# Two attention units and one layer product put into a written-out order at the end of a four-part residual kernel

## The chip, the cores and the metric

The kernel runs on one core of a Trainium2 chip. Its time is the device time of one execution in microseconds (us). The kernel before took 1401.56 us as the median of three runs (1401.19 to 1403.05). Engines are named as in the profile: PE (TensorE, matmuls), DVE (VectorE), ACT (ScalarE), POOL (GpSimd), SP (SyncE, which issues most DMAs; SPq is its queue).

## The reference

`x` is 8 sequences of 128 rows and 512 columns. Four residual layers follow each other:

```
x = x + L0(x)   gated MLP (512 -> 1376 -> 512) with low-rank adapters chosen per sequence
x = x + L1(x)   attention: 32 query heads, 8 key heads, D = 128, q/k RMS norm, rotary,
                512 cached keys from pages + 128 new keys, output projection Wo
x = x + L2(x)   x @ w_eff.T, w_eff = quantised weight (codebook, scales) + low-rank term, 512x512
x = x + L3(x)   x @ weight[adapter].T, one 512x512 matrix per sequence
```

## The kernel before

Every engine has its own queue, written by hand, and engines meet only by semaphores: a wait holds everything that stands behind it on that engine. All products are made in three parts: an operand is split into a high part (`*_h`, by an ACT copy to fp32r) and a low part (`*_l`, the rest, by a DVE or POOL subtraction), and PE multiplies h*h, h*l and l*h.

Layer L1 is cut into 64 units (8 key heads by 8 sequences, `Unit(k)`, k = 0 to 63). A unit goes through: projection of q, k, v; rotary (POOL); `scores(u, h)` for 4 query heads into the PSUM banks `sc0` and `sc1`; `mask_max(u, h)` on DVE, which adds the mask, writes `p_sb` and takes the row maximum (`top`); `shift(u, pair)` on DVE (`bias` from `top` and `rstd`); `exp(u, h)` on ACT; `transpose_p(u, c)` for 5 chunks of 128 keys into `ring0`/`ring1`; `high_pt` (ACT) and `low_pt` (DVE) that split each chunk; `attend(u, c)`, which sums the chunks in `o_ps`; `norm_o` (DVE, times `inv_wide`, which `lay_inv` on ACT writes from `inv_row`); `high_o` and `low_o`; `output(u)`, 12 matmuls into `proj_ps`; and `add_y(u)` (DVE), which adds to `x_sb`. `inv_row` comes by two DMAs of SP, one after the other: `put_inv` (2 KB to DRAM) and `spread_inv` (back to all partitions).

`step(u)` on each engine holds the work of up to four neighbouring units in a fixed order, and `run_steps` calls it for k = 2 up to 66, so that the last steps run with stages of units 62 and 63 alone. `before` is unit 62 and `last` is unit 63 in what follows.

Then come layers L2 and L3, sequence by sequence (b = 0 to 7): `turn_x` transposes `x_sb[b]`, `high_x2`/`low_x2` split it, `layer2(b)` is 12 matmuls, `add3(b)` adds, `turn_x(b, 1)` transposes again, `high_x3`/`low_x3` split, `layer3(b)` is 12 matmuls, `add4(b)` adds, and SP stores `out[b]`. The weights of L2 (1 MB, `w2_raw`) are loaded in one DMA behind the last `spread_inv` and split in one ACT and one DVE instruction; those of L3 are loaded for each sequence (1 MB, two buffers) and split by `high_w3` (ACT) and `low_w3` (DVE). PE waits for all of unit 63, its `add_y` too, ahead of `layer2(0)`.

In the trace the lines of these helpers are: scores L1490, transpose_p L1508, attend L1530, output L1546, L1549 and L1557, layer2 and layer3 L1235, turn_x L1657; mask_max L2021, shift L2037, low_pt L2054, norm_o L2062, low_o L2068, add_y L2074, add3 L2188, add4 L2193, low_w3 L2197, low_x2 L2202, low_x3 L2207, the split of w2 L1206 and L2212; exp L1003, high_pt L1014, high_v L1023, lay_inv L1032, high_o L1042, high_w3 L1190, high_x2 L1196, high_x3 L1202; on POOL rstd L726 and split_v (`vl`) L651; on SP put_inv L533, spread_inv L538, load_v L478 and the loads of w2, w3 and the stores L344. The trace leaves buffer numbers out (`sc`, `ring`), and calls w2 and w3 `w_raw`, `w_h`, `w_l`.

Of the kernel before, what the change touches and what calls it, by code (L numbers as in the profile page):

```python
# [106 lines left out]
def run_steps(step, first):  # L107


    for k in range(first, UNITS + DEPTH - 1):  # L110
        step(Unit(k))
# [17 lines left out]
def cond_resid_kernel(nc, ins, out):  # L129
    ctx = ExitStack()  # L130
    with ctx:
# [29 lines left out]
        down_ps = [o_ps[:, :], proj_ps[:, :]]  # L161
# [87 lines left out]
        p_sb = l1_sb("p_sb", [P, 6, KEYS])  # L249
# [92 lines left out]
        def _(sp):  # L342
# [230 lines left out]
        def _(pool):  # L573
# [164 lines left out]

            pool.wait_ge(S["iota_set"], 7)
            run_steps(step, 0)  # L740


        @block.scalar
        def _(act_e):
# [436 lines left out]
            run_steps(step, 2)  # L1181


            def high_w3(b):
                act_e.wait_ge(w3_load[b % 2], 16 * (b // 2 + 1))
                if b < 2:
                    act_e.wait_ge(S["y"], UNITS)
                else:
                    act_e.wait_ge(S["l3_done"], b - 1)
                act_e.activation(w3_h[:, b % 2, :, :], w3_raw[:, b % 2, :, :], ACT.Copy).then_inc(S["w3_hi"], 1)  # L1190

            def high_x2(b):
# [3 lines left out]
                act_e.activation(x2T_h[:, b % 2, :], ring[0][:, :], ACT.Copy).then_inc(S["xT_hi"], 1)  # L1196
# [7 lines left out]
            act_e.wait_ge(S["kv_done"], UNITS)  # L1204
            act_e.wait_ge(S["w2_in"], 48 * C + 16)
# [3 lines left out]
            for b in range(B):  # L1209
# [8 lines left out]
        def _(pe):  # L1218
# [414 lines left out]
            run_steps(step, 2)  # L1633


            def layer3(b):
# [17 lines left out]

            def turn_x(b, slot, name):
                for c in range(C):
                    i = nc.tensor.transpose(ring[slot][:, c * P:(c + 1) * P], x_sb[:, b, c * P:(c + 1) * P], ident[:, :])  # L1657
                i.then_inc(S[name], 1)

            pe.wait_ge(S["ptl"], UNITS * KC)  # L1660
            pe.wait_ge(S["y_added"], UNITS - B + 1)
            turn_x(0, 0, "xT_done")
            pe.wait_ge(S["y_added"], UNITS)
            for b in range(B):
                layer2(b)
                if b + 1 < B:
                    turn_x(b + 1, 0, "xT_done")
                if b:
                    layer3(b - 1)
                pe.wait_ge(S["x3_added"], b + 1)  # L1670
                turn_x(b, 1, "x3T_done")
# [4 lines left out]
        def _(dve):  # L1676
# [333 lines left out]
            def mask_max(u, h):  # L2010
# [7 lines left out]
                if u.back(ago):  # L2018
# [164 lines left out]
            run_steps(step, 2)  # L2183
# [103 lines left out]
```

## Time and profile before

| | before |
|---|---|
| median of 3 runs | 1401.56 us |
| the profiled execution | 1401.19 us, its span 1399.5 us, mean granted TensorE clock 0.996 |
| PE busy over the span | 1370.9 us (98%) |
| DVE / ACT / POOL busy | 1023.3 (73%) / 977.6 (70%) / 751.3 us (54%) |
| PE busy in 1310 to 1330 us | 15.81 of 20 us |
| PE busy in 1330 to 1340 us | 6.64 of 10 us |
| PE busy in 1340 to 1350 us | 6.99 of 10 us |
| PE busy in each 10 us from 1350 to 1390 us | 10.00 |

A time in the trace is counted from the start of the span; 1.69 us of the execution lie outside the span. The granted clock is given as a share of full speed; it is 1.00 in each of these stretches. An idle time in brackets stands at the instruction that ended it, with the releaser.

### The profile page before, as it was taken

Reading aid. Unit: us, or ns where it says so; the run is one execution under the profiler, and the core shown is the slowest. Engines: PE = TensorE matmul, PEld = TensorE weight load, DVE = VectorE, ACT = ScalarE, POOL = GpSimd, SP = SyncE. Lnnn points to the kernel's source line nnn. Section 1 sums busy time; section 2 is a strip of 40 time slices with the busy share of each in tenths; the row PEclk is TensorE's granted clock in tenths of the full one; section 3 lists DMA queues with packets and bytes.
Section 4 is the critical chain, followed back from the end, with each engine's and each line's share of the span. In section 5 each row is a group of like instructions: output and inputs, shape, how many; then the busy total and the mean of one; then the engine's idle time right before and its main releaser. Section 6 shows DMA issues by size and latency. Waiting matters only on the chain.

```text
span 1399.5 us, 26373 instructions
## 1 busy us (share of the span) xinstructions
PE 1370.9 (98%) x7830; PEld 1189.5 (85%) x7830; DVE 1023.3 (73%) x2112; ACT 977.6 (70%) x1986; POOL 751.3 (54%) x986
## 2 busy tenths in 40 slices
PE   9999999899999999999999999999999999999888
PEld 7878877788888888888888888888888888888766
DVE  4877776677777777777777777777777777777666
ACT  5757665577776677777777777777777777767643
POOL 5421323666765576557655665666566656655300
PEclk9999999999999999999999999999999999999999
DMA  7986889466334233524333334232424243332154
GB/s 194 269 282 178 273 269 286 110 140 170 92 64 106 61 91 65 118 68 96 64 106 62 91 61 106 61 92 63 115 59 108 62 110 71 82 61 61 32 187 151
DMA packets 256596, 165.80 MB, mean 118 GB/s; under 512 B 157398, under 2 KB 223575, under 8 KB 250951
## 3 DMA queue, kind: packets, MB, share of 16 engines
q1 hardware_dynamic: 249808, 142.48, 39.3%
q0 software_dynamic: 5376, 19.60, 5.1%
q10 hardware_dynamic: 1270, 2.04, 0.4%
q8 instruction: 64, 1.05, 0.3%
q14 instruction: 78, 0.63, 0.2%
HBM read 158.66 MB, written 38.94 MB: 141 GB/s over the span
## 4 chain that ended last, share of the span: by engine, by line
PE 77%; SPq 5%; POOL 4%; ACT 4%; DVE 4%; issue 3%; DMA 2%; POOLq 0%; ACTq 0%; DVEq 0%
PE proj_ps L1453 17%; PE sc L1490 15%; PE o_ps L1530 14%; PE ring L1508 9%; PE proj_ps L1546 4%; PE proj_ps L1549 4%; PE proj_ps L1557 4%; SPq L344 2%; PE o_ps L1235 2%; PE proj_ps L1235 2%; PE ring L1569 2%; SPq L381 2%; ACT wb L808 1%; POOL q_sin L680 1%; POOL q_cos L691 1%
## 5 line engine op out<-in xcount | busy, mean ns | idle before, releaser
L2054 DVE TENSOR_TENSOR pTl<-ring,pTh 128x512 fp32r<-128x512 f32 x320 | 215.2, 689 | 140.4 <-ACT pTh L1014 136.0
L1003 ACT ACTIVATE p_sb<-p_sb,bias,rstd 128x640 f32<-128x640 f32 x256 | 235.2, 919 | 57.5 <-DVE bias L2037 57.5
L726 POOL TENSOR_TENSOR rstd<-var,half_neg 128x4 f32<-128x4 f32 x64 | 68.8, 1076 | 304.9 <-DVE var L2086 304.9
L2021 DVE CUSTOM_DVE_ANT_0 p_sb<-sc,mask 128x640 f32<-128x640 f32 x256 | 206.0, 823 | 30.3 <-PE sc L1490 24.6
L1014 ACT ACTIVATE pTh<-ring 128x512 fp32r<-128x512 f32 x320 | 184.6, 600 | 29.5 <-PE ring L1508 27.9
L1508 PE MATMUL ring<-ident,p_sb 128*128 128x128 f32 x1280 | 181.5, 272 | 4.2 <-DVE pTl L2054 2.7
L1508 PEld LDWEIGHTS ring<-ident,p_sb 128*128 128x128 f32 x1280 | 152.8, 140 | 31.2 <-DVE pTl L2054 3.4
L1453 PE MATMUL proj_ps<-wh,xh 128*128 128x256 f32 (+1 forms) x484 | 168.6, 348 | 0.0
L1490 PE MATMUL sc<-kTh,qTh 128*128 128x320 f32 x512 | 163.0, 318 | 0.0
L1453 PE MATMUL proj_ps<-wl,xh 128*128 128x256 f32 (+1 forms) x484 | 161.9, 334 | 0.0
L1453 PE MATMUL proj_ps<-wh,xl 128*128 128x256 f32 (+1 forms) x484 | 161.7, 334 | 0.0
L1490 PE MATMUL sc<-kTh,qTl 128*128 128x320 f32 x512 | 158.4, 309 | 0.0
L1490 PE MATMUL sc<-kTl,qTh 128*128 128x320 f32 x512 | 158.1, 309 | 0.0
L1050 ACT ACTIVATE q_sb<-proj_ps 128x512 f32<-128x512 f32 x64 | 38.3, 598 | 170.9 <-PE proj_ps L1453 162.3
L634 POOL DMA_DIRECT2D v_pages<-in_v_cache x128 | 65.4, 511 | 142.6 <-issue 141.4
L680 POOL TENSOR_TENSOR q_sin<-q_sb,rope 128x256 f32<-128x256 f32 x128 | 92.6, 745 | 76.8 <-issue 72.5
L1530 PE MATMUL o_ps<-pTh,vh 128*128 128x512 f32 x256 | 116.9, 457 | 0.0
L1530 PE MATMUL o_ps<-pTl,vh 128*128 128x512 f32 x256 | 101.5, 397 | 0.0
L1490 PEld LDWEIGHTS sc<-kTh,qTh 128*128 128x128 f32 x512 | 96.6, 189 | 5.3
L1490 PEld LDWEIGHTS sc<-kTl,qTh 128*128 128x128 f32 x512 | 96.6, 189 | 5.2
L1530 PE MATMUL o_ps<-pTh,vl 128*128 128x512 f32 x256 | 101.0, 394 | 0.0
L1453 PEld LDWEIGHTS proj_ps<-wh,xh 128*128 128x128 f32 x484 | 91.4, 189 | 10.9
(264 smaller groups left out, 3633.8 us busy)
## 6 DMA issues: line engine op xcount, KB each, us to landing
v_pages<-in_v_cache POOLq DMA_DIRECT2D x128, 128.0 KB, 3.9
k_pages<-in_k_cache SPq DMA_DIRECT2D x128, 128.0 KB, 3.6
k_raw<-k_pages SPq DMA_DIRECT2D x256, 64.0 KB, 2.6
v_raw<-v_pages SPq DMA_DIRECT2D x64, 256.0 KB, 4.2
rope<-rope_dram SPq DMA_DIRECT2D x64, 256.0 KB, 3.8
inv_row<-inv_dram SPq DMA_DIRECT2D x64, 256.0 KB, 4.0
stage<-in_Wqkv SPq DMA_DIRECT2D x32, 384.0 KB, 4.9
w_raw<-in_WguT SPq DMA_DIRECT2D x19, 512.0 KB, 5.1
```

The costliest lines, as they stand in the source:

```text
L634: pool.dma_start(v_pages[b, j * PSIZE:(j + 1) * PSIZE, :, :].rearrange("s h d -> s (h d)"), ins["v_cache"][bass.ds(pg, 1), :, :, :].rearra ...
L680: pool.tensor_tensor(dst[:, :, s, :], src[:, :, 1 - s, :], tab[:, 1, s * 64:(s + 1) * 64].unsqueeze(1).to_broadcast([P, REP, 64]), ALU.mul ...
L726: pool.tensor_tensor(rstd[:, u.k % 2, 0:REP], var[:, u.k % 2, 0:REP], half_neg[:, 0:REP], ALU.pow).then_inc(S["q_pow"], 1)
L1003: act_e.activation(p_sb[:, p_slot(u, h), :], p_sb[:, p_slot(u, h), :], ACT.Exp, bias=bias[:, h:h + 1], scale=rstd[:, u.k % 2, h:h + 1], ac ...
L1014: act_e.activation(pTh[:, c, :], ring[c % 2][:, :], ACT.Copy).then_inc(S["pth"], 1)
L1235: i = mm(out, a, b, start=start and k == 0, stop=stop and k == last)
L1453: i = mm(proj_ps[:, 0:width], a[:, b, c, :], w[:, c, cols:cols + width], start=k == 0, stop=k == 3 * C - 1)
L1490: i = mm(score_ps[h % 2][:, s, 0:SPLIT], a[:, par, hs], w[:, par, ks], start=k == 0, stop=k == 2)
L1508: i = nc.tensor.transpose(ring[c % 2][:, h * P:(h + 1) * P], p_sb[:, p_slot(u, h), c * P:(c + 1) * P], ident[:, :])
L1530: i = mm(o_ps[:, :], a, w[:, c, :], start=c == 0 and k == 0, stop=c == KC - 1 and k == 2)
L2021: v.tensor_tensor_reduce(out=p_sb[:, p_slot(u, h), :].rearrange("p (s k) -> p s k", s=2), in0=score_ps[h % 2][:, :, 0:SPLIT], in1=mask[:, ...
L2054: v.tensor_tensor(pTl[:, c, :], ring[c % 2][:, :], pTh[:, c, :].bitcast(F32), ALU.subtract).then_inc(S["ptl"], 1)
```

## The change

The last steps (k = 64 to 66) are taken out of the loop on PE, DVE and ACT and written out by hand, mixed with the beginning of L2 and L3:

- PE: `scores(last, 2)` and `scores(last, 3)` come ahead of the third transposed chunk of unit 62; the transposes of `x_sb[0]` and `x_sb[1]` come ahead of unit 63's first chunk; `output(before)` comes behind the first two chunks of unit 63; `layer2(0)` comes ahead of `output(last)`.
- L2 writes to other PSUM banks: its transposes to the halves of `sc0` (two, in turn), its product to the first half of `sc1`. L3 keeps `proj_ps` and `ring1`.
- `p_sb` has 8 slots in place of 6, and unit 63 puts its heads 2 and 3 in the new ones, so that they need not wait until unit 62 is transposed.
- w2 is loaded by SP as soon as unit 63's k and v are projected, ahead of the steps 64 to 66; ACT splits it in four pieces (`high_w2(c)`) between the exps and the chunks of unit 62, and POOL makes the low parts in four pieces (`low_w2(c)`) between its `split_v(62)` and `split_v(63)`. The DVE instruction for it goes.
- The first w3 is loaded after step 64, the second after step 66.
- At the end `turn_x(7)` stands in the middle of `layer3(6)`, cut in two halves.

```diff
-            run_steps(step, 0)
-            sp.wait_ge(S["kv_done"], UNITS)
-            load(w2_raw[:, :, :], w2_dram, S["w2_in"])
-            for b in range(B):
+            run_steps(step, 0, UNITS)
+            sp.wait_ge(S["kv_done"], UNITS)
+            load(w2_raw[:, :, :], w2_dram, S["w2_in"])
+            run_steps(step, UNITS, UNITS + 1)
+            load_w3(0)
+            run_steps(step, UNITS + 1)
+            for b in range(1, B):
+                load_w3(b)
...
             pool.wait_ge(S["iota_set"], 7)
-            run_steps(step, 0)
+            run_steps(step, 0, UNITS)
+            for c in range(C):
+                low_w2(c)
+            run_steps(step, UNITS)
...
-            act_e.activation(w2_h[:, :, :], w2_raw[:, :, :], ACT.Copy).then_inc(S["w2_hi"], 1)
+            def high_w2(c):
+                if c == 0:
+                    act_e.wait_ge(S["kv_done"], UNITS)
+                    act_e.wait_ge(S["w2_in"], 48 * C + 16)
+                act_e.activation(w2_h[:, c, :], w2_raw[:, c, :], ACT.Copy).then_inc(S["w2_hi"], 1)
...
+            high_o(third_last)
+            high_q(last)
+            exp(before, 1)
+            high_new_k(last)
+            high_v(before)
+            high_w2(0)
+            high_w2(1)
+            exp(before, 2)
+            exp(before, 3)
...
+            high_pt(before, 4)
+            lay_inv(before)
+            exp(last, 2)
+            exp(last, 3)
+            high_o(before)
...
+            transpose_p(before, 0)
+            transpose_p(before, 1)
+            scores(last, 2)
+            scores(last, 3)
+            transpose_p(before, 2)
...
+            attend(before, 4)
+            turn_x2(0)
+            turn_x2(1)
+            transpose_p(last, 0)
+            transpose_p(last, 1)
+            output(before)
+            transpose_p(last, 2)
...
+            attend(last, 4)
+            layer2(0)
+            output(last)
+            turn_x3(0)
...
+            layer3(B - 2, 0, 2)
+            turn_x3(B - 1)
+            layer3(B - 2, 2, C)
             layer3(B - 1)
...
-                if u.back(ago):
+                if u.back(ago) and p_slot(u, h) < 6:
...
+            low_pt(before, 1)
+            mask_max(last, 2)
+            low_pt(before, 2)
+            mask_max(last, 3)
+            shift(last, 1)
+            low_pt(before, 3)
...
+            add3(0)
+            low_w3(0)
+            add_y(last)
+            low_x3(0)
+            low_w3(1)
```

On PE, from the second chunk of unit 62 on (L1508 and L1560 are transpose_p, L1530 and L1582 attend, L1490 and L1542 scores of unit 63), the order before is:

```order
L1508 MATMUL ring1<-ident,p_sb 128x128 [waits knl]
L1508 MATMUL ring1<-ident,p_sb 128x128 x3
L1508 MATMUL ring0<-ident,p_sb 128x128 [waits ptl]
L1508 MATMUL ring0<-ident,p_sb 128x128 x3
L1530 MATMUL o_ps<-pTh,vh 128x512 [waits vnl_set,ol,vl_set,pth]
...
L1530 MATMUL o_ps<-pTl,vnh 128x512 [waits ptl]
L1490 MATMUL sc0<-kTh,qTh 128x320 [waits topped]
...
L1546 MATMUL proj_ps<-woh,oTh 128x512 [waits y_added,oh]
```

and with the change it is:

```order
L1560 MATMUL ring1<-ident,p_sb 128x128 [waits knl]
L1560 MATMUL ring1<-ident,p_sb 128x128 x3
L1542 MATMUL sc0<-kTh,qTh 128x320 [waits topped]
...
L1542 MATMUL sc1<-kTh,qTh 128x320 [waits topped]
...
L1560 MATMUL ring0<-ident,p_sb 128x128 [waits ptl]
L1560 MATMUL ring0<-ident,p_sb 128x128 x3
L1582 MATMUL o_ps<-pTh,vh 128x512 [waits vnl_set,ol,vl_set,pth]
```

The 12 score matmuls have moved from behind the last attend of unit 62 to the place ahead of its third chunk, where PE waits for `ptl`.

On PE at the end of unit 63 (L1546 to L1557 and L1598 to L1609 are output, L1235 and L1287 layer2, L1657 turn_x), the order before is:

```order
L1530 MATMUL o_ps<-pTl,vnh 128x512 [waits ptl]
L1546 MATMUL proj_ps<-woh,oTh 128x512 [waits y_added,oh]
...
L1557 MATMUL proj_ps<-wol,oTh 128x512 x4
L1657 MATMUL ring0<-ident,x_sb 128x128 [waits y_added,ptl]
L1657 MATMUL ring0<-ident,x_sb 128x128 x3
L1235 MATMUL o_ps<-w2_h,x2T_h 128x512 [waits w2_lo,xT_lo,y_added]
```

and with the change it is:

```order
L1582 MATMUL o_ps<-pTl,vnh 128x512 [waits ptl]
L1287 MATMUL sc1<-w2_h,x2T_h 128x512 [waits w2_lo,xT_lo]
...
L1598 MATMUL proj_ps<-woh,oTh 128x512 [waits y_added,oh]
...
L1609 MATMUL proj_ps<-wol,oTh 128x512 x4
L1712 MATMUL ring1<-ident,x_sb 128x128 [waits ptl,x3_added]
```

The first layer product stands ahead of the output projection and no longer waits for unit 63's sum; the transpose it needs was made before unit 63's chunks.

On ACT around the exps of unit 62's heads 2 and 3 (L1020 is exp, L1040 high_v, L1223 the split of w2), the order with the change is:

```order
L1040 ACTIVATE vh<-v_raw 128x512 [waits pv,v_load]
L1223 ACTIVATE w2_h<-w2_raw 128x512 [waits w2_in,kv_done]
L1223 ACTIVATE w2_h<-w2_raw 128x512
L1020 ACTIVATE p_sb,total<-p_sb,bias,rstd 128x640 [waits biased] x2
L1223 ACTIVATE w2_h<-w2_raw 128x512
```

Two pieces of w2 and the wait for its DMA now stand ahead of those exps; before, the exps followed high_v at once.

## Rows read from the trace of the kernel before

**Rows 1.** The page's head: the span and its instructions.

```profile
span 1399.5 us, 26373 instructions
```

**Rows 2.** Timeline of PE: start, us, instruction, idle before and releaser.

```profile
1314.87 0.66 PE L1508 MATMUL ring<-ident,p_sb 128*128 128x128 f32 x4 [1.73 <-DVE pTl L2054]
...
1326.08 1.09 PE L1508 MATMUL ring<-ident,p_sb 128*128 128x128 f32 x8 [1.48 <-ACT p_sb L1003]
1328.15 0.66 PE L1508 MATMUL ring<-ident,p_sb 128*128 128x128 f32 x4 [0.98 <-DVE pTl L2054]
...
1335.50 1.19 PE L1546 MATMUL proj_ps<-woh,oTh 128*128 128x512 f32 x4 [2.30 <-ACT oTh L1042]
...
1342.25 0.47 PE L1235 MATMUL o_ps<-w_h,x2T_h 128*128 128x512 f32 x1 [3.32 <-DVE x2T_l L2202]
...
1347.11 0.50 PE L1235 MATMUL o_ps<-w_h,x2T_h 128*128 128x512 f32 x1 [0.41 <-DVE x2T_l L2202]
...
1393.32 0.50 PE L1235 MATMUL proj_ps<-w_h,x3T_h 128*128 128x512 f32 x1 [1.41 <-DVE x3T_l L2207]
```

**Rows 3.** The chain of waits in order of time: start, us, what.

```profile
1307.58 0.93 PE proj_ps L1546 x4
...
1313.11 0.74 DVE p_sb L2021
...
1319.90 1.77 PE sc L1490 x12
...
1326.26 1.38 DMA inv_dram<-inv
...
1327.66 5.22 DMA inv_row<-inv_dram
...
1350.13 0.44 PE ring L1657 x4
...
1353.77 2.77 PE o_ps L1235 x12
...
1385.84 2.77 PE o_ps L1235 x12
```

**Rows 4.** Timeline of DVE, three places.

```profile
1040.61 1.52 DVE L2037 SCALAR_TENSOR_TENSOR bias<-top,rstd 128x2 f32<-128x2 f32 x1
...
1316.19 0.69 DVE L2054 TENSOR_TENSOR pTl<-ring,pTh 128x512 fp32r<-128x512 f32 x1 [0.78 <-ACT pTh L1014]
...
1342.07 2.28 DVE L2197 TENSOR_TENSOR w_l<-w_raw,w_h 128x2048 fp32r<-128x2048 f32 x1
```

**Rows 5.** Timeline of POOL, two places.

```profile
1040.26 1.86 POOL L658 TENSOR_TENSOR wl<-stage,wh 128x768 fp32r<-128x768 f32 x1 [1.31 <-ACT wh L867]
...
1312.93 1.27 POOL L651 TENSOR_TENSOR vl<-v_raw,vh 128x512 fp32r<-128x512 f32 x1
```

**Rows 6.** Timeline of ACT.

```profile
1310.07 0.92 ACT L1003 ACTIVATE p_sb<-p_sb,bias,rstd 128x640 f32<-128x640 f32 x1 [1.19 <-DVE bias L2037]
...
1312.73 1.09 ACT L1014 ACTIVATE pTh<-ring 128x512 fp32r<-128x512 f32 x2 [0.74 <-PE ring L1508]
1314.25 0.92 ACT L1003 ACTIVATE p_sb<-p_sb,bias,rstd 128x640 f32<-128x640 f32 x1 [0.43 <-DVE bias L2037]
...
1318.34 1.12 ACT L1032 ACTIVATE q_sin<-inv_row 128x512 f32<-128x512 f32 x1
```

**Rows 7.** Timeline of SP's DMA issues, the `inv_row` of unit 62.

```profile
1314.23 0.32 SPq L538 DMA_DIRECT2D inv_row<-inv_dram  x1
```

**Rows 8.** DMA issues: count, KB each, median us from issue to landing.

```profile
inv_row<-inv_dram SPq DMA_DIRECT2D x64, 256.0 KB, 4.0
...
w_raw<-in_W3T SPq DMA_DIRECT2D x8, 1024.0 KB, 5.4
...
w_raw<-w_dram SPq DMA_DIRECT2D x1, 1024.0 KB, 7.4
...
prep<-scale_dram SPq DMA_DIRECT2D x2, 256.0 KB, 10.4
```

More of the change, by code:

```diff
@@ L104, in heads, with run_steps @@
         return self.k // B * per + n
-def run_steps(step, first):
-    for k in range(first, UNITS + DEPTH - 1):
+def run_steps(step, first, last=UNITS + DEPTH - 1):
+    for k in range(first, last):
         step(Unit(k))
@@ L1653, in layer2, with turn_x @@
                       ).then_inc(S["l2_done"], 1)
-            def turn_x(b, slot, name):
+            def turn_x(b, bank):
                 for c in range(C):
[L1657 to L1663, printed above, removed]
@@ L1664, in _, with turn_x2, turn_x3 @@
-            for b in range(B):
+                    i = nc.tensor.transpose(bank[:, c * P:(c + 1) * P], x_sb[:, b, c * P:(c + 1) * P], ident[:, :])
+                return i
+            def turn_x2(b):
+                pe.wait_ge(S["y_added"], UNITS - B + b + 1)
+                if b < 2:
+                    pe.wait_ge(S["topped"], UNITS * REP)
+                else:
+                    pe.wait_ge(S["xT_lo"], B + b - 1)
+                turn_x(b, turn2_ps[b % 2]).then_inc(S["xT_done"], 1)
+            def turn_x3(b):
+                pe.wait_ge(S["x3_added"], b + 1)
+                if b == 0:
+                    pe.wait_ge(S["ptl"], UNITS * KC)
+                else:
+                    pe.wait_ge(S["x3T_lo"], b)
+                turn_x(b, ring[1]).then_inc(S["x3T_done"], 1)
@@ new lines, in _ @@
+            before, last = Unit(UNITS - 2), Unit(UNITS - 1)
+            transpose_p(before, 0)
[3 more added lines that the diff above has]
+            transpose_p(before, 2)
+            attend(before, 0)
+            transpose_p(before, 3)
+            attend(before, 1)
+            transpose_p(before, 4)
+            attend(before, 2)
+            attend(before, 3)
+            attend(before, 4)
+            turn_x2(0)
+            turn_x2(1)
@@ L1665, in _ @@
+            transpose_p(last, 0)
+            transpose_p(last, 1)
+            output(before)
+            transpose_p(last, 2)
+            attend(last, 0)
+            transpose_p(last, 3)
+            attend(last, 1)
+            transpose_p(last, 4)
+            attend(last, 2)
+            attend(last, 3)
+            attend(last, 4)
+            layer2(0)
+            output(last)
+            turn_x3(0)
+            for b in range(1, B):
                 layer2(b)
                 if b + 1 < B:
-                    turn_x(b + 1, 0, "xT_done")
@@ L2208, in low_x3 @@
                                 ).then_inc(S["x3T_lo"], 1)
-            dve.wait_ge(S["y_added"], UNITS)
-            dve.wait_ge(S["w2_hi"], 1)
-            v.tensor_tensor(w2_l[:, :, :], w2_raw[:, :, :], w2_h[:, :, :].bitcast(F32), ALU.subtract).then_inc(S["w2_lo"], 1)
-            low_x2(0)
+            before, last = Unit(UNITS - 2), Unit(UNITS - 1)
+            mean_square_q(last)
+            invert(before)
+            mask_max(last, 0)
+            mask_max(last, 1)
+            shift(last, 0)
+            low_pt(before, 0)
+            low_pt(before, 1)
[4 more added lines that the diff above has]
+            low_pt(before, 3)
+            low_pt(before, 4)
+            norm_o(before)
+            invert(last)
+            low_o(before)
+            low_pt(last, 0)
+            low_pt(last, 1)
+            low_x2(0)
+            low_x2(1)
+            add_y(before)
+            low_pt(last, 2)
+            low_pt(last, 3)
+            low_pt(last, 4)
+            norm_o(last)
+            low_o(last)
+            add3(0)
             low_w3(0)
-            for b in range(B):
+            add_y(last)
+            low_x3(0)
+            low_w3(1)
+            for b in range(1, B):
                 add3(b)
```

84 lines of the change are left out of this document (56 added, 28 removed).

## The prediction, made before the changed kernel ran

> **What bounds the kernel now.** I read the page's head first [rows 1]: the change can touch only the end of a span of 1399.5 us. Then the timeline of PE from 1310 us on, for the instructions that come after an idle time [rows 2]. PE, which is otherwise busy without a break, stands still, in its six longest waits up to 1347.11: 1.73 us (unit 62's third chunk waits for `ptl` on DVE), 1.48 (unit 63's first chunk waits for the exps), 0.98 (`ptl` again), 2.30 (output of unit 63 waits for `oTh`), 3.32 (`layer2(0)` waits behind `add_y`, the 2.3 us split of w2 and `low_x2` on DVE) and 0.41. That is 10.22 us. One more wait of 1.41 us stands ahead of the last product. From 1353.77 to 1385.84 five sequences of L2 and L3 pass in 32.07 us, 6.41 each, and PE never waits [rows 3]. So PE's in-order work sets the end, and the most that a new order can win is these 11.6 us, plus the slow start of matmuls after a wait.
>
> **The change part by part.** I lay the new order out with the durations of the trace. All PE work is kept: the same matmuls, in other places and banks.
>
> Scores ahead of chunk 3. `scores(63, 2)` needs the maximum of head 0, `scores(63, 3)` that of head 1, whose mask instruction stands in the chain from 1313.11 on, behind the read-out of head 0, and takes 0.74 [rows 3]. So the first can start at about 1313.15 and finds the second maximum ready. They take 1.77 us [rows 3] and end at about 1315.0; before, chunk 3 started at 1314.87 [rows 2]. So the first wait is filled, at a cost of 0.1. The five chunks and attends then take what they took, 1319.90 - 1314.87 = 5.03 us [rows 2, 3], to 1320.05. DVE now has `mask_max(63, 2)` and `(63, 3)`, 0.74 us each, between the `low_pt`s. The first fits in the 0.78 us that DVE was idle ahead of 1316.19 [rows 4], the second delays `low_pt(62, 3)` to about 1318.1, needed only at 1318.85. The masks no longer stand behind `norm_o`.
>
> The exps of unit 63. ACT runs `exp(63, 0)` at 1314.25 as before [rows 6], then chunk splits and `exp(63, 1)` in turn (two splits took 1.09, an exp 0.92), and reaches `lay_inv(62)` at 1318.5 where it was at 1318.34 [rows 6]. `lay_inv` takes 1.0 of ACT's time and two exps 2 x 0.92 and a read-out of 0.1, 1.95, so the last is done at 1321.5. It needs `inv_row`: issued at 1314.23 [rows 7] and landing 4.0 later as a rule [rows 8], at 1318.2. Now a w3 load of 1 MB is issued some 1.6 us behind it (behind `v_raw` and the read of an adapter index; my estimate). The bounds are 4.0 (not disturbed) and 5.2 (5.22 for the last `inv_row` from 1327.66, with 3 MB issued behind it [rows 3]). I take 4.4, near the first, since the disturber comes later and is one third: 0.25 us. Chunk 1 of unit 63 starts at 1321.75, where it was 1326.08 [rows 2]. PE fills the time from 1320.05 with two transposes of `x_sb`, 0.44 each [rows 3], and is idle for 0.8.
>
> From there PE has no wait that I can find: two chunks 0.95, `output(62)` 3 x 0.93 = 2.79 [rows 3] (its `oTh` is ready at 1322.3, while the chunks run), 5.03, `layer2(0)` 2.77, `output(63)` 2.79, a transpose 0.44. Sum 14.77; `layer2(1)` starts at 1336.52, before at 1347.11 [rows 2]. Gain 10.6 us.
>
> What hides the rest. The 2.30 wait: `norm_o`, `high_o`, `low_o` of unit 63 take 2.1 us in a row beside `layer2(0)`'s 2.77. Their `inv_row` is issued at 1321.7 + 1.4 [rows 3] or up to 0.6 later, lands by 1328.9 even at 5.2, and `lay_inv` could begin as late as 1330.3 before it costs anything. The 3.32 wait: w2's split is done long before. Its pieces on ACT: the load goes out when unit 63's k and v are projected, about 1300.5; at 5.4 (w3's row) it lands at 1305.9, at its own 7.4 (3 MB in flight then) at 1307.9 [rows 8]. ACT is idle for 1.19 us ahead of 1310.07 [rows 6], two pieces need 1.0, so they are free if it lands by 1309.05; piece 3 runs in the 0.74 us that ACT waited ahead of unit 62's first chunk at 1312.73, piece 4 ends at 1314.2 and meets `exp(63, 0)` at 1314.25. POOL does its four low parts at about 1.27 us each (as the `vl` of the same size, [rows 5]) from 1314.2 to 1319.3; they are needed at 1330.3.
>
> What POOL's pieces do to DVE. A 128x2 `bias` on DVE took 1.52 us from 1040.61, to 1042.13, and POOL's subtraction from 1040.26 took 1.86, to 1042.12 [rows 4, 5]: DVE was held until POOL's instruction ended. `shift(63, 1)` at 1317.7 now meets the third of four such instructions, which ends at about 1318.0: 0.3 us, hidden. The bounds are nothing and 1.27 us if one has just begun. The Trainium skill, page SBUF — State Buffer, section Who interferes with whom, says a DVE instruction with two SBUF inputs and a GpSimd one that reads SBUF exclude each other for the whole instruction, and who issues first decides; the trace agrees by that 1.52. Neither says who comes next when POOL has another one waiting; that is a rival below.
>
> The layer loop. In the first round, `low_w3(1)` (2.28 us, [rows 4]) stands ahead of `add3(1)` and `low_x2(2)` on DVE. `high_w3(1)` ends at about 1339.1, `low_w3(1)` at 1341.4, `add3(1)` at 1342.0 (needed at 1342.5), `low_x2(2)` at 1342.65 (needed at 1342.95). It fits with 0.3 to spare; below that it costs what is missing. Then the loop is the old one, 6.41 per sequence. The old first round took 1353.77 - 1347.11 = 6.66 after a wait, so 0.25 more is won. At the end: from `layer2(7)` to the last product took 1393.32 - 1385.84 = 7.48; now 2.77 + 1.38 + 0.44 + 1.38, and then `add4(6)` and `low_x3(7)` in a row on DVE, 1.38: 7.35, 0.1 won. The 1.41 wait stays, in effect, since `add4(6)` now stands between.
>
> Sum: 10.6 + 0.25 + 0.1 = 10.95 us. Against the profiled execution (span 1399.5 us [rows 1] plus 1.69, 1401.19) this gives 1390.24. The median of the runs is 0.37 above that execution, so I predict 1390.6 us.
>
> **The rivals.**
> 1. The loads crowd each other. w3's first 1 MB goes out right after `v_raw` of unit 63 and about 1.6 us after `inv_row` of unit 62, its second about 1.2 after `inv_row` of unit 63. If `inv_row` takes w2's 7.4 [rows 8], `lay_inv(62)` starts at 1321.65 rather than 1318.7: 3.0 us more on the exps. At 5.2 it is 0.8 more than my sum. For it: the 5.22 from 1327.66 [rows 3], where 1 MB loads follow. Against it: there they were three, here it is one. Time 1391.4 to 1393.6.
> 2. DVE is late in the first layer round, by `high_w3(1)` standing behind `high_x3(0)`. For it: only 0.3 us to spare behind a 2.28 us instruction. Each 1 us late costs 1; with a w3 that comes 1 to 2 us late, 1391.5 to 1392.5.
> 3. POOL keeps its place through all four pieces. `shift(63, 1)` then runs at 1319.3, `low_pt(62, 3)` ends at 1320.0 and unit 62's last attend at 1321.1 in place of 1320.05; with two transposes 1322.0 against 1321.75 for the exps: 0.3 us more, 1390.9. Rows that have a `bias` beside POOL's back-to-back work are none here, so I give it a small chance; it barely moves the time.
> 4. The idle times only move: PE stands in order, and a wait on the last exp or on `pth` comes back between chunks in place of the old ones, so that less than 2.8 us is won. For it: 0.98 us between chunks 2 and 3 was such a wait. Against it: `output(62)` now covers that one, and no producer in my layout is later than its use but the exps. 1400.
> 5. Slower: ACT is held by the load of w2, a wait that stood behind all exps and now stands ahead of `exp(62, 2)`. Everything behind it, unit 62's and 63's exps and chunks and so PE, shifts by landing minus 1309.05. At the longest row of the DMA groups, 10.4 [rows 8], that is 1.9 us: 1392.5, still faster. It ends slower only if the landing is after 1320, 19.5 us after issue, 21 us giving 1402.1. No row is near.
>
> **How the numbers follow.** My forecast (1389.2 to 1391.4) 0.62; rival 1: 0.17; rival 2: 0.09; rival 3: 0.05; rival 4: 0.03; rival 5: 0.02 on the slow side and 0.02 for its small price. The low end is my sum without the 0.25 for `inv_row`, without the 0.8 idle and the 0.1 of the scores: 1389.4, less 0.4 for the scatter of executions, 1389.0. The high end takes in rival 1's whole price with some of rival 2: 1394.5. What can be told from no change here is 0.2%, 2.8 us: faster than 1398.8 has 0.95, within it 0.03, slower 0.02.
>
> **What would show it.** In the changed profile: scores starting near 1313.2 and chunk 3 near 1315.0, with no wait of 1.7; one PE wait, below 1.2 us, ahead of unit 63's first chunk at 1321.6 to 1322; `layer2(0)` and `output(63)` back to back from about 1330.3; `layer2(1)` at 1336.5 and a period of 6.41; the split of w2 on ACT at 1308.8 without a wait for DMA; span 1388.6. The prediction is wrong if PE's waits after 1310 sum to more than 4 us, if ACT waits for w2, or if the rest of the span, which is not changed, takes another time.

## The result, and the profile after

| | before | changed |
|---|---|---|
| median of the runs, us | 1401.38 (1398.61 to 1403.05, 4 runs) | 1388.11 (1386.92 to 1390.87, 4 runs) |
| profiled execution, us | 1401.19 | 1388.78 |
| its span, us | 1399.5 | 1387.1 |
| reciprocal of unit 62 on DVE, us into the span | 1312.02 | 1309.76 |
| from there to the end of the span (the tail) | 87.48 | 77.34 |

The ratio of the runs is 0.9913, 95% interval 0.9896 to 0.9931: 9.7 to 14.6 us faster (the quotient of the two medians alone is 0.9905). 1390.6 was predicted, in a range of 1389.0 to 1394.5, so the median lies 0.9 us below the low end (by the ratio, 0.9913 of the 1401.56 us that it was reckoned from, it is 1389.4, just inside). In a later call the same kernel took 1389.19 (6 runs, ratio 0.9918, 0.9903 to 0.9933). Two executions at a lower granted clock, 1942.89 us of the kernel before and 1494.91 us of e11, are left out of every median and ratio here.

The two spans differ by 12.4 us, but the change shows only behind the reciprocal of unit 62 (`inv`, whose transfers to `inv_row` begin the tail). That instruction stands 2.26 us earlier in the changed kernel's trace. The reciprocal of unit 1 and that of unit 62, in the kernel before, then in the changed one:

```profile
286.08 0.17 DVE L2047 RECIPROCAL inv<-total 128x4 f32<-128x4 f32 x1
...
1312.02 0.18 DVE L2047 RECIPROCAL inv<-total 128x4 f32<-128x4 f32 x1
```

```profile
283.96 0.17 DVE L2145 RECIPROCAL inv<-total 128x4 f32<-128x4 f32 x1
...
1309.76 0.18 DVE L2145 RECIPROCAL inv<-total 128x4 f32<-128x4 f32 x1
```

2.12 of the 2.26 us are there 286 us into the span, a thousand us ahead of the first changed instruction. Between the two rows pass 1025.94 and 1025.80 us. So 2.26 us is scatter of the first 286 us. TensorE's granted clock is one thing that differs there: it was 0.72 from 216 to 220 us and 0.85 from 220 to 224 before, and 1.00 in both in the changed kernel. In the eleven further traces the reciprocal of unit 62 stands between 1307.47 and 1312.14. Two things of the change do stand ahead of it, the load of w2 and ACT's first two pieces, but they hold nothing back: from ACT's read of unit 63's `k_sb`, when the load goes out, to that reciprocal pass 11.50 us before (from 1300.52) and 11.51 changed (from 1298.25). The change is worth the 10.14 us by which the tail is shorter, in this pair of traces. I compare tails from here on, since whole runs of one kernel differ by 2 to 9 us. Add 2.26 to a time of the changed trace to set it beside a time of [rows 2].

The medians say some 13 us, 3 more than the tails. Over all runs at hand the kernel before took 1401.6 us on average at a mean granted clock of 0.995 (47 runs beside the experiments), the changed kernel 1389.1 at 0.997 (10 runs): 12.5 us. The difference of clock is of the size of the 2.4 us that are left (with 1.00 and 0.50 as its levels, a mean lower by 0.002 is some 2.8 us of lost work over such a span; an estimate). Where in those runs it fell is not known, as only the profiled executions have a trace. It can be scatter ahead of the change, or a fall behind the long waits of the old tail, as in e5 and e9 below; in that case the change is worth more than 10.14 us in such runs. That stays open.

PE in the changed kernel, all instructions with an idle time before them from 1308 us on (start us, us, line, operation; in brackets the idle time and what ended it). They answer to the seven of [rows 2]:

```profile
1319.15 1.09 PE L1560 MATMUL ring<-ident,p_sb 128*128 128x128 f32 x8 [0.55 <-ACT p_sb L1020]
...
1377.50 0.66 PE L1712 MATMUL ring<-ident,x_sb 128*128 128x128 f32 x4 [1.30 <-DVE x_sb L2286]
...
1380.93 0.50 PE L1287 MATMUL proj_ps<-w_h,x3T_h 128*128 128x512 f32 x1 [1.38 <-DVE x3T_l L2305]
```

Of 11.63 us of waits (11.97 with one of 0.34 at 1346.04, which those rows leave out) 3.23 are left. The first is the one predicted (0.8, ahead of unit 63's first chunk). The second is new. The chain of waits (start us, us, what), which answers to [rows 3]:

```profile
1310.90 2.03 PE sc L1542 x12
1312.93 0.44 PE ring L1560 x4
...
1327.80 2.72 PE sc L1287 x12
1330.53 0.91 PE proj_ps L1598 x4
...
1333.69 2.76 PE sc L1287 x12
...
1372.62 1.92 ACT w_h L1205
...
1374.56 0.36 DVE w_l L2295
1374.92 1.85 issue
1376.77 0.69 DVE x_sb L2286
```

Three things stand in these rows. The scores of unit 63 stand ahead of chunk 3, without a wait. `layer2(0)` at 1327.80 and `output(63)` at 1330.53 pass without a gap. And at 1372.10, where `layer2(7)` starts, the chain leaves PE for the first time since 1319.15: it goes through ACT's split of the last w3, DVE's split of it, and `add3(7)`. DVE there (before, its order was the same: the split of w3 at 1388.31, 2.29 us, then `add3(7)` at 1390.52):

```profile
1374.56 2.29 DVE L2295 TENSOR_TENSOR w_l<-w_raw,w_h 128x2048 fp32r<-128x2048 f32 x1 [1.11 <-ACT w_h L1205]
1376.77 0.68 DVE L2286 TENSOR_TENSOR x_sb<-x_sb,sc 128x512 f32<-128x512 f32 x1
1379.59 0.69 DVE L2291 TENSOR_TENSOR x_sb<-x_sb,proj_ps 128x512 f32<-128x512 f32 x1 [2.14 <-PE proj_ps L1287]
1380.19 0.68 DVE L2305 TENSOR_TENSOR x3T_l<-ring,x3T_h 128x512 fp32r<-128x512 f32 x1
```

### The profile page after: what moved, and what is told of

It is laid out like the page before. It is cut to its first block, busy times and chain, and to the rows that moved or that the text cites. A ratio compares the mean times of both kernels' runs of the same rounds, so it can differ in the third digit from the quotient of the medians.

```text
span 1387.1 us, 26390 instructions
## 1 busy us (share of the span) xinstructions
PE 1367.5 (99%) x7830; PEld 1187.9 (86%) x7830; DVE 1022.0 (74%) x2111; ACT 976.7 (70%) x1989; POOL 755.6 (54%) x990
## 4 chain that ended last, share of the span: by engine, by line
PE 78%; SPq 5%; POOL 5%; ACT 4%; DVE 3%; issue 3%; DMA 1%; POOLq 0%; ACTq 0%; DVEq 0%
PE proj_ps L1505 17%; PE sc L1542 15%; PE o_ps L1582 14%; PE ring L1560 9%; PE proj_ps L1598 4%; PE proj_ps L1601 4%; PE proj_ps L1609 4%; SPq L349 3%; PE proj_ps L1287 2%; PE sc L1287 2%; PE ring L1621 2%; SPq L386 2%; ACT wb L825 1%; POOL q_sin L689 1%; POOL q_cos L700 1%
## 5 line engine op out<-in xcount | busy, mean ns | idle before, releaser
L1020 ACT ACTIVATE p_sb<-p_sb,bias,rstd 128x640 f32<-128x640 f32 x256 | 235.2, 919 | 54.2 <-DVE bias L2135 54.1
L1560 PE MATMUL ring<-ident,p_sb 128*128 128x128 f32 x1280 | 181.4, 272 | 0.8 <-ACT p_sb L1020 0.5
L1560 PEld LDWEIGHTS ring<-ident,p_sb 128*128 128x128 f32 x1280 | 153.0, 140 | 27.2 <-ACT p_sb L1020 1.0
L1542 PE MATMUL sc<-kTh,qTh 128*128 128x320 f32 x512 | 162.7, 318 | 0.0
L1542 PE MATMUL sc<-kTh,qTl 128*128 128x320 f32 x512 | 158.1, 309 | 0.0
L1542 PE MATMUL sc<-kTl,qTh 128*128 128x320 f32 x512 | 157.8, 308 | 0.0
L1582 PE MATMUL o_ps<-pTh,vh 128*128 128x512 f32 x256 | 116.9, 456 | 0.0
L1582 PE MATMUL o_ps<-pTl,vh 128*128 128x512 f32 x256 | 101.6, 397 | 0.0
L1542 PEld LDWEIGHTS sc<-kTh,qTh 128*128 128x128 f32 x512 | 96.3, 188 | 5.5 <-DVE top L2119 0.3
L1582 PE MATMUL o_ps<-pTh,vl 128*128 128x512 f32 x256 | 101.0, 394 | 0.0
L1542 PEld LDWEIGHTS sc<-kTl,qTh 128*128 128x128 f32 x512 | 96.3, 188 | 5.2
```

Of the source, the lines that this page charges most:

```text
L1020: act_e.activation(p_sb[:, p_slot(u, h), :], p_sb[:, p_slot(u, h), :], ACT.Exp, bias=bias[:, h:h + 1], scale=rstd[:, u.k % 2, h:h + 1], ac ...
L1542: i = mm(score_ps[h % 2][:, s, 0:SPLIT], a[:, par, hs], w[:, par, ks], start=k == 0, stop=k == 2)
L1560: i = nc.tensor.transpose(ring[c % 2][:, h * P:(h + 1) * P], p_sb[:, p_slot(u, h), c * P:(c + 1) * P], ident[:, :])
L1582: i = mm(o_ps[:, :], a, w[:, c, :], start=c == 0 and k == 0, stop=c == KC - 1 and k == 2)
```

## The experiments

Each is an edit of the changed kernel (tail 77.34; 77.42 when it was traced again) and leaves the output as it is. The theory: PE's order and the places where it waited on DVE or ACT are the whole gain, and one new wait at the end gives 1.3 to 1.5 us of it back. The rivals are those of the prediction, above all that idle time only moves, and that loads hold back the small transfers.

| run | edit | tail, us | against 77.34 | median, us | ratio to before, 95% |
|---|---|---|---|---|---|
| e1_no_cut | layer3(6) in one piece | 76.06 | -1.28 | 1389.15 | 0.9873 to 0.9939 |
| e2_add_first | add3(7) ahead of the last w3 split | 76.01 | -1.33 | 1388.07 | 0.9868 to 0.9937 |
| e3_output_first | layer2(0) behind output(63) | 80.17 | +2.83 | 1391.66 | 0.9909 to 0.9952 |
| e4_unit_order_old | units 62, 63 in the old order | 80.58 | +3.24 | 1392.62 | 0.9907 to 0.9955 |
| e5_w2_late | e3, and w2 (with the first w3) at its old places | 85.44 | +8.10 | 1398.17 | 0.9961 to 0.9985 |
| e9_load_early_split_late | e5, load of w2 early | 85.96 | +8.62 | 1397.14 | 0.9954 to 0.9978 |
| e6_w3_crowd | both w3 loads ahead of inv_row(62) | 84.66 | +7.32 | 1396.34 | 0.9951 to 0.9978 |
| e7_end_only | e2, layer3(7) in a free bank | 74.43 | -2.91 | 1385.85 | 0.9874 to 0.9912 |
| e8_end_and_loads | e7, first two w3 loads early | 74.25 | -3.09 | 1384.87 | 0.9867 to 0.9904 |
| e10_after_again | none | 77.42 | +0.08 | 1389.19 | 0.9903 to 0.9933 |
| e11_best_again | e8 again, beside e10 | 74.23 | -3.11 | 1386.45 | 0.9875 to 0.9916 |

**The end of the layer loop.** e1 gives back the old end:

```diff
-            layer3(B - 2, 0, 2)
+            layer3(B - 2)
             turn_x3(B - 1)
-            layer3(B - 2, 2, C)
```

> The changed kernel with its last product before the end whole again: the transpose of x_sb[7] stands behind layer3(6), not in the middle of it. Theory A (in the changed kernel add3(7) stands behind the 2.29 us split of the last w3 on DVE, so the transpose in the middle makes PE wait 1.30 us where the second half of layer3(6) could have run): PE's wait ahead of the transpose falls from 1.30 to about 0.05, layer3(6) ends 1.3 us earlier, the span is 1.2 to 1.4 us shorter. Theory B (the cut is worth its 0.1 us, as I predicted, and the 8.83 us from layer2(7) to layer3(7) come from something else): the span is 0 to 0.1 us longer.

e2 keeps the cut and changes DVE's order alone:

```diff
-                add4(b - 1)
-                low_x3(b)
-                if b + 1 < B:
+                if b < B - 1:
+                    add4(b - 1)
+                    low_x3(b)
+                if b + 2 < B:
                     low_w3(b + 1)
+            low_w3(B - 1)
+            low_x3(B - 1)
+            add4(B - 2)
```

> The changed kernel, cut kept, with DVE's last round in another order: add3(7) ahead of the split of the last w3, and low_x3(7) ahead of add4(6). Theory A (DVE's order is what makes the cut cost): no wait ahead of the transpose of x_sb[7], layer3(7) starts about 7.0 us after layer2(7) in place of 8.83, the span is 1.8 us shorter. Theory B (the wait has another cause, ACT or the w3 load): no more than 0.7 us shorter.

PE's waits near the end of e1, then of e2:

```profile
1381.97 0.50 PE L1287 MATMUL proj_ps<-w_h,x3T_h 128*128 128x512 f32 x1 [1.41 <-DVE x3T_l L2304]
```

```profile
1319.78 1.09 PE L1560 MATMUL ring<-ident,p_sb 128*128 128x128 f32 x8 [0.95 <-ACT p_sb L1020]
...
1379.82 0.47 PE L1287 MATMUL proj_ps<-w_h,x3T_h 128*128 128x512 f32 x1 [1.08 <-DVE x_sb L2291]
```

In e1 the wait of 1.30 is gone, and `layer3(7)` starts 7.48 us after `layer2(7)` (1374.49 in the chain), as before the change. So the cut, which was to win 0.1, cost 1.3. In e2 it is 7.04 (from 1372.78), 1.79 less than the changed kernel's 8.83, as expected. Its tail is only 1.33 shorter since the exps were 0.4 later: `put_inv(62)` took 2.50 there and `inv_row` came 0.28 too late for ACT. So differences of tails below some 0.4 us are not to be read. The medians of whole runs do not resolve these two edits: e1's 1389.15 and e2's 1388.07, against 1388.11.

**layer2(0) ahead of output(63).** e3:

```diff
-            layer2(0)
             output(last)
+            layer2(0)
```

> The changed kernel with layer2(0) behind output(63) again, all else kept. Theory A (the product in front hides norm, high and low part of unit 63's output, and its own add): PE waits 1.4 us for oTh, and about 0.7 more for add3(0) ahead of the next transpose: 2.1 us longer. Theory B (the early load and split of w2 alone took the waits of 2.30 and 3.32 away): within 0.3 us of the changed kernel.

```profile
1328.99 1.20 PE L1598 MATMUL proj_ps<-woh,oTh 128*128 128x512 f32 x4 [1.42 <-ACT oTh L1059]
...
1335.51 0.66 PE L1712 MATMUL ring<-ident,x_sb 128*128 128x128 f32 x4 [0.78 <-DVE x_sb L2286]
```

Two new waits, 2.20 us together, for `oTh` and for `add3(0)`. The tail grew by 2.83, 0.7 more than theory A had it, because a wait costs some 0.3 us beyond its own length: these products take 0.39 us and start 0.23 apart, an overlap that a wait ends, and the first four behind it take 1.20 us (1.07 without a wait, as at 1330.36 in the changed kernel). The old 2.30 wait for `oTh` [rows 2] is what `layer2(0)` covers.

**The order of units 62 and 63.** e4 puts scores, exps, masks and output(62) back to their old places on PE, ACT and DVE. On PE:

```diff
-            scores(last, 2)
-            scores(last, 3)
             transpose_p(before, 2)
...
+            scores(last, 2)
+            scores(last, 3)
+            output(before)
...
-            output(before)
```

> The changed kernel with units 62 and 63 in the old order on PE, ACT and DVE (scores of heads 2 and 3, their masks and exps behind unit 62's attends, output(62) ahead of unit 63's chunks), the two x_sb transposes in the wait for the exps, and everything from unit 63's third chunk on as changed. Theory A: the waits of 1.73 and 0.98 us and part of the 1.48 come back, since output(62) covers nothing and the masks stand behind norm_o: layer2(1) starts 3.2 us later, the time is 3.2 us longer. Theory B (most of the gain is at the seam to the layers, the unit order only moves idle time): under 1 us longer.

```profile
1313.96 0.66 PE L1560 MATMUL ring<-ident,p_sb 128*128 128x128 f32 x4 [1.73 <-DVE pTl L2152]
...
1325.18 1.09 PE L1560 MATMUL ring<-ident,p_sb 128*128 128x128 f32 x8 [0.61 <-ACT p_sb L1020]
1327.25 0.66 PE L1560 MATMUL ring<-ident,p_sb 128*128 128x128 f32 x4 [0.97 <-DVE pTl L2152]
```

The waits of 1.73 and 0.98 of [rows 2] are back, at 1.73 and 0.97. The two `x_sb` transposes stay at their new place in this edit. The idle time did not just move (rival 4): where an order takes it out, the tail is shorter by it.

**The load and the split of w2.** e5 is e3 with the load back behind `spread_inv(63)` (the first w3 load behind it too), and one split each on ACT and DVE in place of four pieces:

```diff
+            run_steps(step, UNITS)
             load(w2_raw[:, :, :], w2_dram, S["w2_in"])
-            run_steps(step, UNITS, UNITS + 1)
-            load_w3(0)
-            run_steps(step, UNITS + 1)
...
+            add_y(last)
+            dve.wait_ge(S["w2_hi"], 1)
+            v.tensor_tensor(w2_l[:, :, :], w2_raw[:, :, :], w2_h[:, :, :].bitcast(F32), ALU.subtract).then_inc(S["w2_lo"], 1)
```

> The changed kernel with layer2(0) behind output(63), as in the run that moved that one step, and with the last w2's load and split back in one piece at their old places: the load behind spread_inv(63), one instruction each on ACT and DVE behind the load, no pieces on POOL; the rest as changed. The same output. Measure: from the reciprocal of unit 62 on DVE to the end of the span (before 87.48 us, changed kernel 77.34, with output first 80.17). Account to be tested: 10.14 in all = 3.24 (unit order) + 2.83 (layer2(0) ahead of output) - 1.28 (the cut at the end, which cost) + x, so x, the early load and split of w2, is 5.35. Theory A, the four parts add up: the tail is 5.3 longer than with output first alone, 85.5, and the PE has a wait of 4 to 5 us ahead of layer2(0), put down to DVE w_l. Rival (rival 4 of the prediction, idle only moves): the parts overlap, an early w2 is worth under 4 us once output stands first, tail under 84.2.

e9 differs from e5 by the load of w2 alone, which stands ahead of `run_steps(step, UNITS)` as in the changed kernel.

> As the run with the load and split of w2 back at their old places (tail 85.44 us, layer2(0) behind output(63)), but with the load of w2 early, where the changed kernel has it, before step 64. The splits stay in one piece each, ACT's behind the read-out of unit 63, DVE's behind add_y(63). The same output. It divides the 5.3 us of that part into the load and the place of the split. Theory A (the place of the split in DVE's order, behind add_y(63), is all of it; the load had landed when ACT came to the split at 1331.23, which waited for no DMA): tail 85.0 to 85.8, PE waits about 3.1 us for w_l ahead of layer2(0). Rival: with the load early, ACT or DVE reach the split sooner, tail 83 or less.

The two longest of PE's waits in e5, then in e9:

```profile
1331.24 1.20 PE L1593 MATMUL proj_ps<-woh,oTh 128*128 128x512 f32 x4 [1.95 <-ACT oTh L1055]
1337.35 0.76 PE L1282 MATMUL sc<-w_h,x2T_h 128*128 128x512 f32 x1 [3.08 <-DVE w_l L2332]
```

```profile
1326.99 1.20 PE L1593 MATMUL proj_ps<-woh,oTh 128*128 128x512 f32 x4 [1.42 <-ACT oTh L1055]
1333.07 0.76 PE L1282 MATMUL sc<-w_h,x2T_h 128*128 128x512 f32 x1 [3.07 <-DVE w_l L2332]
```

Both tails came out close to theory A (85.44 against 85.5, and 85.96, 0.16 above its 85.0 to 85.8), but e5's not by the sum that stands in the expectation. The wait is 3.08, not 4 to 5; the rest is the clock. PE in e5, then before (stretch, its length, PE busy, granted clock as a share of full speed, DMA share, GB/s):

```profile
1336.00:1337.00 1.00, 0.00 (x0) 1.00 0.00 0
1337.00:1338.00 1.00, 0.65 (x2) 0.55 0.00 0
1338.00:1339.00 1.00, 1.00 (x4) 0.50 0.00 0
1339.00:1340.00 1.00, 1.00 (x3) 0.50 0.00 0
```

```profile
1342.00:1343.00 1.00, 0.75 (x3) 1.00 0.00 0
```

The first seven of the twelve matmuls of `layer2(0)` in e5, and all twelve in e9, run at half clock (1.2 GHz), most of them 0.63 us long where a full-speed one takes 0.39 to 0.40. From the start of `layer2(0)` to `add3(0)` on DVE passed 4.49 us in e5 (to 1341.84), 5.50 in e9 (to 1338.57), 3.05 in the kernel before (1342.25 to 1345.30): the clock cost 1.44 and 2.45. Without it the tails are 84.00 and 83.51. So of what w2's part is worth beyond e3, 3.8 us, the place of the split is 3.3 (DVE does it in one piece behind `add_y(63)`, which waits for the output; what its form and its engine are worth by themselves was not run) and the early load 0.5 (in e5 `lay_inv(63)` waits 0.81 for `inv_row`, in e9 it does not).

The account is then 3.24 + 2.83 + 3.83 - 1.28 = 8.62 of the 10.14 us. The other 1.5 are in no experiment, but the traces show where most of them lie. No run put the transposes of `x_sb[0]` and `x_sb[1]`, or L2's PSUM banks, back. In the kernel before, `low_x2(0)` stands on DVE behind the split of w2, and between `layer2(0)` and `layer2(1)` PE waits twice, 0.41 for `low_x2(1)` [rows 2] and, ahead of the transpose for L3:

```profile
1346.04 0.65 PE L1657 MATMUL ring<-ident,x_sb 128*128 128x128 f32 x4 [0.34 <-DVE x_sb L2188]
```

From the start of `output(63)` to `layer2(1)` passed 11.61 us there (1335.50 to 1347.11), in e5 10.32 (1331.24 to 1343.00, less 1.44 for the clock). The 1.29 between them belong to the early transposes and the banks, and the wait ahead of `output(63)` is 0.35 shorter (1.95 for 2.30). This part is read from traces and not shown by a run of its own. The sum of 10.14 in the expectation took its last term, 5.35, as what was left; e5's 5.27 met it because the fall of the clock (1.44), which the trace of before does not have, stood in for these 1.5.

**Loads in flight.** e6 issues both first w3 loads (2 MB) between `put_inv(62)` and `spread_inv(62)`:

```diff
+                if u.k == UNITS:
+                    sp.wait_ge(S["inv_put"], (u + -2).count(16, 16))
+                    load_w3(0)
+                    load_w3(1)
                 spread_inv(u + -2)
...
-            run_steps(step, UNITS, UNITS + 1)
-            load_w3(0)
-            run_steps(step, UNITS + 1)
-            for b in range(1, B):
+            run_steps(step, UNITS)
+            for b in range(2, B):
```

> The changed kernel with both first w3 loads (2 MB) issued between put_inv(62) and spread_inv(62) rather than behind inv_row(62). The same output. Tests rival 1, that loads in flight hold back the small transfers of the reciprocals. If they do: inv_row(62) lands 7 us after its issue rather than 4.0, lay_inv(62) on ACT waits about 3 us for it, chunk 1 of unit 63 waits some 3 us more on PE than its 0.55, and the tail is 79.5 to 80.5. If not: lay_inv(62) waits under 0.5 us, and the tail is within 0.5 of 77.34.

SP's queue in e6, ACT's `lay_inv(62)`, and PE:

```profile
1310.45 0.32 SPq L538 DMA_DIRECT2D inv_dram<-inv  x1
1313.48 1.45 SPq L349 DMA_DIRECT2D w_raw<-in_W3T  x2
1314.98 0.43 SPq L543 DMA_DIRECT2D inv_row<-inv_dram  x1
```

```profile
1322.46 1.11 ACT L1051 ACTIVATE q_sin<-inv_row 128x512 f32<-128x512 f32 x1 [5.70 <-DMA inv_row<-inv_dram]
```

```profile
1325.43 1.97 PE L1562 MATMUL ring<-ident,p_sb 128*128 128x128 f32 x8 [6.33 <-ACT p_sb L1022]
```

`inv_row` landed 7.5 us after its issue (1314.98 to 1322.46), as the theory of crowding had it, in place of 4.0. But the tail grew by 7.32 and not by 3. The issue itself came 2.3 later (4.74 after the reciprocal, 2.41 in the changed kernel), because two issues of 0.73 stood in front of it and `put_inv` took 3.0; with 3.5 for the landing that makes the 5.8 by which PE's wait grew. And behind the wait the clock was down: from there to the end of the first output product passed 3.32 us (to 1328.75), 1.87 in the changed kernel (1319.15 to 1321.02), 1.45 more. So large loads issued ahead of `inv_row` hold it back, at a price of more than rival 1 had. Rival 1 itself spoke of loads behind it, and there little is seen: with 1 MB issued 1.6 us behind, `inv_row(62)` of the changed kernel landed in 3.8 us (4.0 in e8, without a load beside it); with 3 MB from 0.4 us behind, `inv_row(63)` took 5.2 in the kernel before and 4.8 in e5.

**A better end.** With the cut and the DVE order of e2, `layer3(7)` still waits 1.08 for `add4(6)`, only because both use one PSUM bank. e7 gives it the free `o_ps`, and takes the high products first and those with `x3T_l` last (what each of the two is worth was not run):

```diff
+            def layer3_last():
...
+                    mm(o_ps[:, :], xh3[c], w3_h[:, b % 2, c, :], start=c == 0, stop=False)
+                pe.wait_ge(S["w3_lo"], b + 1)
...
-            layer3(B - 1)
+            layer3_last()
```

> The changed kernel with the cut of the last layer steps kept, add3(7) ahead of low_w3(7) on DVE and low_x3(7) ahead of add4(6), as in the run that did this alone, and further layer3(7) in a PSUM bank that stands free, so that it doesn't wait for add4(6), with its product of the two high parts first. The same output. Theory A (the end is bound by DVE's x_sb ahead of layer3(7)): layer3(7) starts right behind the second half of layer3(6), 6.0 us after layer2(7) starts (changed kernel 8.83, with the DVE order alone 7.04); what then stands behind the last product is as before, so the tail is 74.6 to 75.2 against 76.0. Rival: another wait takes its place, ACT's x3T_h or DVE's w_l inside layer3(7), and the tail stays at 75.7 to 76.2.

e8 further issues w3(0) and w3(1) right behind w2, 14 and 24 us earlier.

> The same as the kernel with the new end (free PSUM bank for layer3(7)), and w3(0) and w3(1) loaded right behind w2, some 15 us earlier, before step 64, so that no load is issued beside the transfers of the two reciprocals. The same output. Theory A (a load in flight lengthens put_inv and inv_row): put_inv(63) to spread_inv(63) takes 1.4 to 2.2 us rather than 3.2, chunk 1 of unit 63 waits no more than 0.6 us, tail 74.4 to 75.0. Rival: the transfers of the reciprocals vary by themselves, the tail is that of the new end alone within 0.3 us; or the loads, now earlier, hold back the transfers of unit 61 or w2, and ACT's pieces wait: tail over 75.5.

The chain at the end of e7, and SP's queue in e8:

```profile
1370.05 2.76 PE sc L1287 x12
1372.81 1.37 PE proj_ps L1287 x6
1374.18 0.44 PE ring L1727 x4
1374.62 1.39 PE proj_ps L1287 x6
1376.01 0.91 PE o_ps L1694 x4
```

```profile
1297.43 1.45 SPq L349 DMA_DIRECT2D w_raw<-in_W3T  x2
...
1317.44 0.32 SPq L538 DMA_DIRECT2D inv_dram<-inv  x1
1320.77 0.32 SPq L543 DMA_DIRECT2D inv_row<-inv_dram  x1
```

In e7 PE has no wait left at the end: 5.96 us from `layer2(7)` to `layer3(7)`, and from `layer2(7)` to the end of the span 11.85 in place of 15.00 (before: 13.66). The tail is 74.43, a little under the 74.6 to 75.2 expected. e8's is 74.25, as expected, but not for my reason: `put_inv(63)` to `spread_inv(63)` took 3.33 us with nothing else in flight, where I expected 1.4 to 2.2. A load in flight does not explain that time; see the last section.

> The changed kernel once more, unedited, so that the version with the new end and early loads is compared with it on the same chip. Every theory expects 1387 to 1390 us and a tail (reciprocal of unit 62 to the end of the span) of 77.0 to 77.9 us, if what I read as effects of 1 us and more in the tails isn't scatter. Rival: tails of the same kernel differ by over 1 us between runs, and then the readings of 1.3 us are not to be trusted.

> The version with add3(7) ahead of low_w3(7), layer3(7) in a free PSUM bank, and w3(0), w3(1) loaded right behind w2, unedited, beside the changed kernel on the same chip. Theory A (the tail is 3.1 us shorter, the rest of the span is the same code): median 2.5 to 3.7 us below the changed kernel's in this call, tail 74.0 to 74.8. Rival (the scatter of whole runs hides it): medians within 1.5 us. Also a second look at put_inv(63) to spread_inv(63), 3.33 us in the first run without a load in flight: if it is again near 3.3, a load in flight is not what lengthens it.

The repeats give 77.42 and 74.23: tails of one kernel agree to 0.1 us, so differences of 1.3 us can be read. In that call the median was 1386.45 for this version and 1389.19 for the changed kernel: 2.7 us less. `put_inv(63)` to `spread_inv(63)` took 2.82 us this time, again with no load in flight. It is the fastest version tried; e7's tail is within 0.2 us of it, so the earlier loads of e8 are not shown to be worth anything.

## Why the prediction was right, and where it was not

Its terms, as times from the reciprocal of unit 62 (the prediction has it at 1312.02):

- **Scores ahead of chunk 3.** Chunk 3 at 3.17, predicted 2.98. Right within 0.2; e4 shows what it is worth with the rest of the unit order.
- **The exps of unit 63.** Chunk 1 of unit 63 at 9.39, predicted 9.73. The 0.25 for a late `inv_row` and 0.1 more did not come: `lay_inv(62)` at 1316.17 waited for nothing, 4.0 after the issue at 1312.17 (`inv_row` had landed 3.8 after it). By the prediction's own 4.4 the price was 0.13 (1318.63 against 1318.5), not 0.25.
- **The stretch without a wait.** `layer2(1)` at 23.93, predicted 24.50; of the 0.57 us, 0.34 is that of the exps, the rest products that follow each other without a gap and so take a little less than the rows behind waits say. The waits of 1.73, 0.98, 2.30, 3.32 and 0.41 us are all gone.
- **w2 in pieces.** ACT's first two pieces stand at 1306.51, without a wait for the load issued at 1298.25; POOL's four took 5.06 us from 1311.91. Rival 5 fell. (Its 21 us come to 1403.05, not 1402.1; no other number hangs on it.)
- **The first layer round.** It passed without a wait, and rival 2 fell: `low_w3(1)` at 1336.16, `add3(1)` at 1338.37, `low_x2(2)` at 1338.97. The period was 6.40, as predicted (6.41).
- **POOL beside DVE.** `shift(63, 1)` on DVE, and POOL's four pieces, of 1.27 us each (columns as above):

```profile
1315.50 0.22 DVE L2135 SCALAR_TENSOR_TENSOR bias<-top,rstd 128x2 f32<-128x2 f32 x1
```

```profile
1311.91 5.06 POOL L750 TENSOR_TENSOR w_l<-w_raw,w_h 128x512 fp32r<-128x512 f32 x4
```

The third piece ends at 1315.71, `bias` at 1315.72, and the fourth piece ends at 1316.97. DVE was not held through the fourth, so rival 3 (POOL keeps its place) fell. In e5, without pieces on POOL, the same instruction took 0.16:

```profile
1316.99 0.16 DVE L2130 SCALAR_TENSOR_TENSOR bias<-top,rstd 128x2 f32<-128x2 f32 x1
```

e9 has 0.16 there too, so the pieces cost it 0.06. The Trainium skill, page SBUF — State Buffer, section Who interferes with whom, has the two engines exclude each other instruction by instruction. The 0.06 fit that: held until the third piece ended, and let through ahead of the fourth.

- **The end of the loop: this term failed.** The prediction had "7.35, 0.1 won" from `layer2(7)` to `layer3(7)`; it was 8.83. It added PE's durations (2.77 + 1.38 + 0.44 + 1.38) and then `add4(6)` and `low_x3(7)`, as if `turn_x(7)` could follow the first half of `layer3(6)` at once. But `turn_x(7)` needs `add3(7)`, and that stands on DVE behind `low_w3(7)`, 2.29 us, which waits for ACT's `high_w3(7)`. Before, the whole `layer3(6)` covered this (`add3(7)` ended at 1391.20, 5.4 us after `layer2(7)` began); half of it does not. The rows for it were in the trace of before. The prediction had checked just this order of DVE for the first round and left it out for the last. e1 and e2 show it from both sides.

In sum: predicted tail 87.48 - 10.95 = 76.53, measured 77.34. The difference of +0.81 is -0.57 to `layer2(1)`, -0.07 in six rounds, +1.48 at the end, and -0.03 behind it and by rounding. The mechanism was right up to the last round, and the win was 0.8 us smaller than forecast. That the median came out 2.5 us below the forecast all the same is no merit of it. The 1401.19 us that it was reckoned from is an execution with a late start of the tail (1312.02 in a spread of 1307.47 to 1312.14), 2.26 of the 2.5 us. The prediction named its own sign for this, the rest of the span taking another time, and the sign came true. It also added 0.37 for the median above the profiled execution, where the changed kernel's median lay 0.67 below it. That the median still lies near the range of 1389.0 to 1394.5 is in part luck: the scatter of the first 286 us is larger than the error of any term.

## What to carry to other kernels

When a step is pulled forward on the bounding engine, write out the order of the engine that feeds it for the same place, in every round in which it stands and above all in the last: the gain of a cut is lost if its input stands behind a long instruction that nobody needs yet. Taking a 2.3 us split out of its late place in DVE's order was worth 3.3 us, loading its data some 24 us earlier 0.5: look at the order first and at the load second, and keep large loads out of the queue between the two halves of a small round trip. To judge an edit at the end of a 1400 us kernel, measure from the last common instruction, not the whole.

## What the runs showed of the hardware that I had not expected

- **A wait's length does not say by itself whether TensorE's clock falls.** A wait of 3.08 us left PE at half clock for the next 3.1 us (e5), one of 3.07 us for 5.5 us (e9), one of 6.33 us for 3.1 us (e6); a wait of 3.32 us in the traced execution of the kernel before left it at 1.00, though 0.98 and 2.30 us of idle time stood close ahead of it too [rows 2]. What makes the difference stays open here. It cost 1.4 to 2.5 us, as much as the waits that this study is about.
- **The 2 KB write of a reciprocal takes 1.4 to 3.4 us,** from its issue to the next one that waits for it: 1.40 and 1.41 (`put_inv(63)` before and in e4), 1.7 to 3.0 for unit 62; for unit 63 in the other kernels 1.9 (e3) to 3.4, with 3.24 in the changed kernel, 3.33 in e8 and 2.82 in e11, where no load was in flight, and 3.38 in e9. Loads in flight do not explain it, and the cause is open.
